# Two key tiles of e and V multiplied in three TensorE blocks in place of four, in a fused attention and feed-forward layer

## The reference

```
Q, K = projections of [x W, conv1d(x W)], V = x Wv
tau, delta = sigmoid(conv(gelu(depthwise conv(x))))            # per head and token
scores = (Q K^T / sqrt(16)) * tau[..., None] + delta[:, :, None, :]
out = softmax(scores) V
x = layernorm(x + out Wo + bo)
x = layernorm(x + mxfp4(x) mxfp4(W)^T + b)
```

## Time and profile before

| | us |
|---|---|
| median of 3 runs | 1803.93 |
| lowest, highest | 1793.26, 1824.42 |
| profiled execution, device time | 1809.25 |
| its span in the trace | 1807.1 |
| mean granted TensorE clock (share of full speed) | 0.941 |

### The profile page before, as it was taken

The page is one execution under the profiler, slowest core; times in us unless marked ns, Lnnn a source line. Parts: engine busy times, 40 slices in busy tenths (PEclk is TensorE's granted clock), DMA queues, the critical chain, the costliest instruction groups (busy, mean ns, idle before and its releaser), DMA issues.

```text
span 1807.1 us, 33772 instructions
## 1 busy us (share of the span) xinstructions
PE 1674.9 (93%) x13869; PEld 749.5 (41%) x13876; DVE 1557.0 (86%) x1654; ACT 1298.7 (72%) x2371; POOL 105.5 (6%) x149
## 2 busy tenths in 40 slices
PE   7999863799999999999999999999999999999765
PEld 6677541233333333333333333333333333334554
DVE  3898545899989999999999989999999999973886
ACT  0666620288878888888888778888888888876323
POOL 4111000200000000000000000000000000010110
PEclk9999985599999999999999989999999999988888
DMA  3344782000050005005100600141150000001331
GB/s 104 81 126 131 154 137 84 1 8 8 8 79 8 8 18 74 8 8 62 24 8 8 82 7 9 25 70 43 42 69 18 8 8 8 14 9 38 111 119 46
DMA packets 45156, 84.65 MB, mean 47 GB/s; under 512 B 8496, under 2 KB 20400, under 8 KB 41904
## 3 DMA queue, kind: packets, MB, share of 16 engines
q1 hardware_dynamic: 43152, 82.48, 21.7%
q10 hardware_dynamic: 1856, 0.09, 0.1%
HBM read 51.36 MB, written 30.67 MB: 45 GB/s over the span
## 4 chain that ended last, share of the span: by engine, by line
PE 60%; DVE 21%; ACT 1%; issue 1%; DMA 1%; SPq 0%; ACTq 0%; POOL 0%; DVEq 0%
PE ps L759 26%; PE ps L746 20%; DVE mx L933 17%; PE ps L731 11%; PE ps L790 1%; DMA out<-o_sb 1%; PE ps L818 1%; ACT y L873 0%; PE ps L723 0%; DVE stats L955 0%; ACT o_sb L873 0%; PE ps L824 0%; PE ps L788 0%; DVE work L981 0%; DVE small L976 0%
## 5 line engine op out<-in xcount | busy, mean ns | idle before, releaser
L896 ACT ACTIVATE e<-ps 128x512 f32<-128x512 f32 x2048 | 1110.3, 596 | 255.8 <-PE ps L746 215.9
L933 DVE TENSOR_REDUCE mx<-ps 128x2 f32<-128x1024 f32 x1024 | 1231.4, 1223 | 63.6 <-PE ps L731 54.4
L759 PE MATMUL ps<-e,v_grp 128*32 128x256 f32 x8192 | 667.9, 398 | 0.2 <-issue 0.2
L746 PE MATMUL ps<-q,k 52*128 52x512 f32 x2048 | 530.9, 506 | 3.6 <-ACT e L896 3.6
L731 PE MATMUL ps<-k,q 50*128 50x512 f32 x2048 | 436.4, 418 | 50.3 <-PEq L363 28.7
L746 PEld LDWEIGHTS ps<-q,k 52*128 52x128 f32 x2048 | 201.3, 186 | 439.3 <-ACT e L896 409.8
L759 PEld LDWEIGHTS ps<-e,v_grp 128*32 128x32 f32 x8192 | 162.7, 108 | 365.5 <-issue 207.0
L731 PEld LDWEIGHTS ps<-k,q 50*128 50x128 f32 x2048 | 204.0, 193 | 87.1 <-DVE mx L933 54.4
L542 PE MATMUL ps<-x_p,m_p 128*128 128x512 f32 x576 | 142.0, 408 | 22.9 <-DVE qx L513 17.8
L542 PEld LDWEIGHTS ps<-x_p,m_p 128*128 128x128 f32 x576 | 111.7, 195 | 56.2 <-DVE qx L513 19.6
L487 DVE SCALAR_TENSOR_TENSOR hid<-x_c,dw_w,hid 128x512 f32<-128x512 f32 x128 | 101.8, 868 | 4.3 <-ACT hid L433 4.1
(11 more groups left out here) (117 smaller groups left out, 660.2 us busy)
## 6 DMA issues: line engine op xcount, KB each, us to landing
k<-k_parts SPq DMA_DIRECT2D x48, 256.0 KB
q<-q_parts SPq DMA_DIRECT2D x48, 256.0 KB
k_parts<-k_sp SPq DMA_DIRECT2D x16, 512.0 KB, 7.3
q_parts<-q_sp SPq DMA_DIRECT2D x16, 512.0 KB, 3.7
att<-ev SPq DMA_DIRECT2D x32, 256.0 KB
x_c<-in_x_t SPq DMA_DIRECT2D x8, 514.0 KB, 7.8
tau_r<-tau_rows SPq DMA_DIRECT2D x16, 256.0 KB
x_in<-in_x SPq DMA_DIRECT2D x8, 512.0 KB, 3.8
```

The costliest lines, as they stand in the source:

```text
L746: nc.tensor.matmul(ps[:, st_bank(n), :], k_set[r, g % 2, jh, kt * P:(kt + 1) * P], q_set[r, g % 2, jh, lo:lo + CH], start=True, stop=True) ...
L759: last = nc.tensor.matmul(ps[32 * h:32 * (h + 1), 0, PVW * part:PVW * (part + 1)], v_grp[:, kt, h, :], e[:, x % E_BUFS, h * CH + PVW * par ...
L896: nc.scalar.activation(e[:, x % E_BUFS, h * CH:(h + 1) * CH], ps[:, st_bank(n), :], ACT.Exp).then_inc(e_ready, 1)
L933: nc.vector.tensor_reduce(mx[:, j % 2, :, jh, qt, kc], ps[:, b0:b0 + 2, :], AX.X, ALU.max).then_inc(s_free, 1)
```

## The change

The two halves of 256 queries per key tile become, over two key tiles, three blocks: 384 queries of the first tile; the other 128 of the first and 128 of the second; the other 384 of the second. Behind the first block stand one score pair and one unit, behind the middle one a score pair, two units and the next tile's first score pair, behind the last a score pair and one unit. `pv_cols` takes a range of columns in place of a half. The insertions of the last iteration move to ends of pairs of tiles.

```diff
-            PVW = CH // 2
+            PVW = 3 * CH // 4
...
-                    def pv_half(i, kt, part):
+                    def pv_cols(i, kt, lo, hi):
...
                         for h in range(HG):
-                            last = nc.tensor.matmul(ps[32 * h:32 * (h + 1), 0, PVW * part:PVW * (part + 1)], v_grp[:, kt, h, :],
-                                                    e[:, x % E_BUFS, h * CH + PVW * part:h * CH + PVW * (part + 1)],
-                                                    start=(kt == 0 and part == 0), stop=(kt == KT - 1 and part == 1), skip_group_check=True)
-                        if part == 1:
+                            last = nc.tensor.matmul(ps[32 * h:32 * (h + 1), 0, lo:hi], v_grp[:, kt, h, :], e[:, x % E_BUFS, h * CH + lo:h * CH + hi],
+                                                    start=(kt == 0 and lo == 0), stop=(kt == KT - 1 and hi == CH), skip_group_check=True)
+                        if hi == CH:
                             last.then_inc(pv_done, 1)
...
-                        for k in range(KT):
-                            x = KT * i + k
-                            for jh in range(HH):
-                                pv_half(i, k, jh)
-                                if x + AHEAD < NIT * KT:
-                                    st(x + AHEAD, jh)
-                                while issued < first + min(due, due * (2 * k + jh + 1) // slots):
-                                    s_item(issued)
-                                    issued += 1
-                            if i == NIT - 1 and k == 1:
+                        def scores(x, jh):
+                            if x < NIT * KT:
+                                st(x, jh)
+
+                        def units(upto, issued):
+                            while issued < first + min(due, due * upto // slots):
+                                s_item(issued)
+                                issued += 1
+                            return issued
+
+                        for k in range(0, KT, 2):
+                            x = KT * i + k + AHEAD
+                            pv_cols(i, k, 0, PVW)
+                            scores(x, 0)
+                            issued = units(2 * k + 1, issued)
+                            pv_cols(i, k, PVW, CH)
+                            pv_cols(i, k + 1, 0, CH - PVW)
+                            scores(x, 1)
+                            issued = units(2 * k + 3, issued)
+                            scores(x + 1, 0)
+                            pv_cols(i, k + 1, CH - PVW, CH)
+                            scores(x + 1, 1)
+                            issued = units(2 * k + 4, issued)
+                            if i == NIT - 1 and k == 0:
                                 ffn_weights()
-                            if i == NIT - 1 and TT - 1 <= k < 2 * TT - 1:
-                                project(0, k - (TT - 1))
-                            if i == NIT - 1 and 2 * TT <= k < 3 * TT:
-                                project(1, k - 2 * TT)
+                            if i == NIT - 1 and TT // 2 <= k // 2 < TT:
+                                for a in (k % TT, k % TT + 1):
+                                    project(0, a)
+                            if i == NIT - 1 and TT <= k // 2 < 3 * TT // 2:
+                                for a in (k % TT, k % TT + 1):
+                                    project(1, a)
```

More of the change, by code:

```diff
@@ L747, in st @@
                                              q_set[r, g % 2, jh, lo:lo + CH], start=True, stop=True).then_inc(st_full, 1)
-                    def pv_half(i, kt, part):
+                    def pv_cols(i, kt, lo, hi):
                         x = KT * i + kt
-                        if part == 0:
+                        if lo == 0:
                             if kt == 0 and i > 0:
```

## The result

The kernel before took 1,804.37 us (median of 16 runs, 1,785.44 to 1,824.42), the changed one 1,828.64 us (16 runs, 1,822.76 to 1,832.05). The medians are 24 us apart. The ratio is 1.0153, 95% interval 1.0128 to 1.0179: slower, but by less than 2%. The ratios in this text leave out runs more than 1.5% above the fastest of their kernel (four of the 16 before, none after); without them the medians here are 27 us apart. The forecast was 1,839 us, +35.

A forecast was written before the change was run, and what follows sets the result against it. TensorE's work with its PV/score switches was taken as the bound, a score-bank wait hidden just behind. 246 pairs of tiles at +0.14 us (34 us), +3 without units, less 1 to 2 at half clock: +35, 1,839 us, range 1,822 to 1,856.

The forecast's parts named there:

- What paces the loop: Attention loop: TensorE's work with its PV/score switches sets the 1.24 us step; VectorE and ScalarE have slack.
- The blocks: PV blocks between score runs: 0.785 us for 384 columns, 0.57 us for 128 + 128.
- The open bound of the short passes: Middle PV block of 128 + 128: 0.57 us if weight loads hide, up to 1.00 if not; low end taken.
- rival 2: Middle PV block's short passes bound by weight loads: up to 1.00 us, 1,945 us at most; chance 0.12.
- The switch: TensorE between PV and scores: one switch back and forth of four gone, a gain of 0.36 us a pair of tiles.
- The bank wait: Second scores behind the middle block wait for a score bank: 1.18 us needed, 0.80 of work, 0.48 us lost.
- B's run: Score pairs and two units behind the middle PV block: 1.61 us in place of 1.13 without waits.
- rival 1: Switches decide, score banks don't: 4.60 us a pair of tiles, 89 us less, 1,715 us; chance 0.12.
- VectorE's wait inside it: Second unit behind the middle block waits for a reduction until 0.82 us, second scores 1.16, ahead of 1.18: free.
- The sum: Whole kernel: 246 pairs of tiles at +0.14 us are 34 us; with the smaller terms +35, median 1,839 us.
- a rival in which it would lose more: TensorE's clock falls more often in the changed loop: 50 us more at half clock cost 20 us, 1,859; chance 0.09.
- Steps without units and the end: End of iteration 30 and all of 31, ten pairs of tiles: +3 us; later output projections counted as nothing.

The follow-up runs named there:

- the first of the three orders: Changed kernel's three PV blocks, with the score pairs and units behind them split so both array row halves work side by side: 1,902.74 us, ratio 1.0563.

## Why the prediction was right or wrong

- **What paces the loop.** Right: with short exponentials and reductions the kernel before keeps 1.24 us a step, so it was TensorE's work with its switches.
- **The blocks.** 0.785 us for 384 columns measured 0.78, 0.57 for 128 + 128 measured 0.57. The open bound of the short passes fell on the low end, as chosen; rival 2 is out.
- **The switch.** 0.36 us a pair of tiles was put down, 0.29 measured with a rest of a wait, about 0.34 without. The gain is real. The Trainium skill ("TensorEngine Tiling (Array Packing)", Key Properties) has the drain at a change of tiling mode, and these runs agree: a change and back is worth 0.29 us, while passes of PV blocks that follow one another in one mode start 0.21 us apart, their streams alone. The bank wait, which turned the gain into a loss, is the kernel's own.
- **The bank wait.** B's run was to take 1.61 us and took 1.62; with short reductions, which take VectorE's wait out, it is 1.62 too. With an exponential of 16 columns it falls to 1.20. This settles rival 1: the switches don't decide while the banks are three.
- **VectorE's wait inside it.** Put at 0.82 and 1.16 us, measured 0.82 and 1.16. It was called free, and is, but it is new in the waits, and with shorter exponentials it decides (1.48 us). (The two reductions of the earlier trace rows start 1.14 us apart, not 1.13 as the prediction has it; nothing hangs on it.)
- **Pair and iteration.** 5.10 us forecast, 5.09 measured; +1.1 us an iteration, measured +1.1.
- **The sum.** Here a term was missing. I set the clock of the kernel before as given and let the changed one keep it, but for 1 to 2 us, with a rival in which it would lose more. It lost less. The kernel before stands 1.7 us where it meets the group's loads and falls to half clock, and loses more behind the reciprocals too; that made it some 10 us slower against the changed kernel than the steps say. Medians 24 us apart in place of 35 are this term in the main; with the loads elsewhere the difference is 33. The term rests on two profiles of each kernel, the clocks of the timed runs and the two runs with late loads; which of the stands holds how much of it stays open.
- **Steps without units and the end.** Not settled: put at +3 us, but the last iteration took 58.1 and 52.0 us before, 56.9 and 55.4 after, with different half-clock stretches in each. One piece can be read. The projections come two at a time now, so TensorE has less work left when ScalarE turns to the first norm (1.2 us of it, 2.6 before). It then stands 4.68 and 4.69 us for an exponential where it stood 3.35 and 3.36. The prediction looked for cover in VectorE's idle time and counted nothing; these 1.3 us are TensorE's.

That iteration 16 recovers sooner in the changed kernel was seen in two profiles of each and not tested by itself. Why the stand near 526 us meets one kernel and not the other was not tested either, but the traces have a likely cause. Both kernels' pages have one more DMA queue, which brings instructions:

```profile
q8 instruction: 105, 1.72, 0.4%
```

In the kernel before 480 and 478 records pass between the start of one packet and that of the next, at 524.16 and 522.69 us, and the stands begin as the late packet ends (525.77 and 524.40 us). In the changed kernel it is 430 and 442 records at this place, with no stand. With late loads the most is 466 and 472, with no such stand either. That TensorE had run out of instructions fits this. It isn't shown: no run changes only the instruction stream's length or place, and the count alone doesn't decide, since the stand of 1.14 us in iteration 12 comes after 406 records.

## What to carry to other kernels

Merging blocks to save TensorE's switches moves other work closer together: before counting the saved switch, write down for each ring of buffers (score banks, unit banks) the shortest distance at which its user may come again, from the release lags in the trace, and lay the new order against it. Here the distance was 1.18 us and the new order left 0.80. And a difference of medians isn't only steps: look where each kernel loses its clock, since a fix there (loads one iteration later, -0.6%) can be worth as much as a rearranged loop.

## What the runs showed that I had not expected

A stand of TensorE of 1.1 to 2.2 us was in most cases followed by half clock, for 3 to 34 us, but not always: 1.53 us with the short reductions, at the reciprocals, and 1.19 us in the first of the three orders were followed by none. At the same place the lengths differed much: behind the reciprocals 17 and 34 us in the kernel before, 7 and 7 in the changed one. And TensorE stood 1.72 to 1.73 us with nothing that it waited for while a group's loads ran, in both profiles of the kernel before at the same unit; with the loads moved by one iteration there was no such stand between 515 and 545 us, nor from 555 to 600, where they then begin.
